# Attention and feed-forward on one core: the last 13 keys of each head as tiles of 32 rows, value products in four banks

## The reference

```python
def block(x, ctx):                                  # per batch
    xn = layernorm(layernorm(x)) * gamma + beta
    q, (k, v) = xn @ w_q, split(ctx @ w_kv)
    p = softmax(q_h @ k_h.T * 64 ** -0.5)           # per head h: 256 x 77
    x = x + (concat(p @ v_h) @ w_out + b_out) * tanh(gate)
    y = layernorm(x)
    h = silu(y @ (w_gate / 127).T) * (y @ (w_up / 127).T)   # 768 hidden
    return x + h @ (w_down / 127).T
```

## Time and profile before

| | us |
|---|---|
| median of 3 runs | 296.05 (295.01 to 296.74) |
| the profiled execution | 297.51 |
| its span | 295.7 |
| PE busy | 285.9 (97%) |
| DVE busy | 231.1 (78%) |
| ACT busy | 158.8 (54%) |
| POOL busy | 172.1 (58%) |
| PE, records of L849 (value products) in the chain that ended last | 10% |

### The profile page before, as it was taken

The page is one execution under the profiler, slowest core; times in us unless marked ns, Lnnn a source line. Parts: engine busy times, 40 slices in busy tenths (PEclk is TensorE's granted clock), DMA queues, the critical chain, the costliest instruction groups (busy, mean ns, idle before and its releaser), DMA issues.

```text
span 295.7 us, 6752 instructions
## 1 busy us (share of the span) xinstructions
PE 285.9 (97%) x2509; PEld 262.9 (89%) x2509; DVE 231.1 (78%) x609; ACT 158.8 (54%) x312; POOL 172.1 (58%) x198
## 2 busy tenths in 40 slices
PE   8999999979999999999999999999999999999895
PEld 7998978868988898989898989898999889988794
DVE  1598887777898789878987897788878878886853
ACT  4646875548268633853484358326842773354142
POOL 2653864358959681966396549635872778145033
PEclk9999999999999999999999999999999999999979
DMA  6995147332432113011201120112012101110001
GB/s 198 384 368 153 34 115 243 147 97 109 145 107 80 24 32 97 0 40 43 73 0 40 42 73 2 39 53 59 3 41 76 35 3 42 41 34 2 0 26 51
DMA packets 26668, 23.32 MB, mean 79 GB/s; under 512 B 12602, under 2 KB 24866, under 8 KB 26634
## 3 DMA queue, kind: packets, MB, share of 16 engines
q1 hardware_dynamic: 26634, 22.86, 24.9%
HBM read 15.87 MB, written 4.62 MB: 69 GB/s over the span
## 4 chain that ended last, share of the span: by engine, by line
PE 86%; DVE 6%; ACT 2%; issue 2%; SPq 1%; DMA 1%; POOL 1%; DVEq 0%
PE ps L904 13%; PE ps L849 10%; PE ps L808 6%; PE ps L816 5%; PE ps L812 5%; PE ps L973 5%; PE ps L977 5%; PE ps L974 5%; PE ps L738 5%; PE ps L831 4%; PE ps L957 3%; PE ps L960 3%; PE ps L925 2%; PE ps L771 1%; PE ps L746 1%
## 5 line engine op out<-in xcount | busy, mean ns | idle before, releaser
L1224 POOL TENSOR_TENSOR probs<-probs,total 128x512 f32<-128x512 f32 x32 | 33.6, 1049 | 59.6 <-DVE total L1363 59.5
L1250 POOL TENSOR_TENSOR h_lo<-hid,h_hi 128x256 fp32r<-128x256 f32 x42 | 30.9, 737 | 29.9 <-ACT h_hi L1137 29.5
L1239 POOL TENSOR_TENSOR t_lo<-t_all,t_hi 128x1232 fp32r<-128x1232 f32 x16 | 45.6, 2852 | 3.8 <-ACT t_hi L1095 3.8
L1067 ACT COPY pt<-ps 128x512 f32<-128x512 f32 x32 | 18.9, 591 | 40.8 <-PE ps L831 40.8
L973 PE MATMUL ps<-wo_hi,o_hi 128*128 128x256 f32 x128 | 36.3, 283 | 0.0
L974 PE MATMUL ps<-wo_lo,o_hi 128*128 128x256 f32 x128 | 36.1, 282 | 0.0
L977 PE MATMUL ps<-wo_hi,o_lo 128*128 128x256 f32 x128 | 36.0, 281 | 0.0
L1083 ACT CAST o_hi<-ps 128x512 fp32r<-128x512 f32 x32 | 17.2, 591 | 27.0 <-PE ps L849 27.0
L1346 DVE TENSOR_REDUCE top<-ps 128x4 f32<-128x308 f32 x64 | 28.7, 473 | 3.4 <-PE ps L816 3.1
L808 PE MATMUL ps<-t_hi,xn_hi 128*128 128x308 f32 x128 | 30.7, 321 | 0.0
L1371 DVE TENSOR_TENSOR o_lo<-ps,o_hi 128x512 fp32r<-128x512 f32 x32 | 20.6, 686 | 12.5 <-ACT o_hi L1083 12.2
(11 more groups left out here) (168 smaller groups left out, 838.2 us busy)
## 6 DMA issues: line engine op xcount, KB each, us to landing
x_ln<-in_x SPq DMA_DIRECT2D x8, 256.0 KB, 2.9
v_scratch<-v_out SPq DMA_DIRECT2D x4, 512.0 KB, 3.3
v_whole<-v_scratch SPq DMA_DIRECT2D x16, 128.0 KB
stream<-in_x SPq DMA_DIRECT2D x8, 256.0 KB, 2.9
x_rooms<-in_x SPq DMA_DIRECT2D x7, 256.0 KB, 7.7
out<-stream SPq DMA_DIRECT2D x7, 256.0 KB, 2.2
wk_raw<-in_L_xattn_w_kv SPq DMA_DIRECT2D x4, 256.0 KB, 5.2
wq_raw<-in_L_xattn_w_q SPq DMA_DIRECT2D x1, 1024.0 KB, 7.9
```

What stands on the lines that cost most here:

```text
L1224: nc.gpsimd.tensor_tensor(whole, whole, scale.to_broadcast([P, HR, HALVES, KEYS_WHOLE]), ALU.mult).then_inc(probs_done, 1)
L1239: nc.gpsimd.tensor_tensor(t_lo[:, :, cols], t_all[:, :, n, cols], t_hi[:, :, cols].bitcast(F32), ALU.subtract).then_inc(tlo_done, 1)
L1250: nc.gpsimd.tensor_tensor(h_lo[:, f, :], hid_of(b, f), h_hi[:, f, :].bitcast(F32), ALU.subtract).then_inc(hlo_done, 1)
```

## The change

The 13 remaining keys of heads 2j and 2j+1 of a group (halves r = 0 and 1) now stand together in 26 of the 32 rows from 32 j on, for j = 0 to 3. Head r's values are in the columns of half e = (r + j) % 2 and zeros in the other half. So a group's 8 rest products use 32 rows and 64 columns each, at eight places of the array. Pair j of a group has a bank of its own: j = 0 takes a bank of the shared ring (V0 and V1 become users of it), j = 1 to 3 take banks 3, 4 and 5. All 8 whole products come first, four and four, then the 8 rest products. The scores have two banks instead of three. o_hi and o_lo are read as 256 and 768 elements per partition instead of 512 twice, and the projection's waits follow. w_out is loaded by four DMAs instead of eight, with its rows in the new order. On DVE, Z2 stands ahead of LN. In the ring, banks are now X1T 6, V0 7, XT 2, G0 6, G1 7, G2 2, G3 6, G4 7, G5 2, V1 6, O0 7, O1 2, D0 6, D1 7; the last rounds have other banks in places.

```diff
-MISC_BANKS = (6, 7, 3)
-SCORE_BANKS = (0, 1, 2)
-LAST_BANKS = (4, 5, 7, 6, 0, 1)
-LAST_X1T_BANKS = (0, 2)
-LAST_DOWN_BANKS = (2, 3)
+MISC_BANKS = (6, 7, 2)
+SCORE_BANKS = (0, 1)
+VALUE_BANKS = (3, 4, 5)
+LAST_BANKS = (4, 5, 2, 6, 0, 1)
+LAST_X1T_BANKS = (0, 3)
+LAST_DOWN_BANKS = (3, 7)
+FORMER_GATE_BANK = 6
...
-DVE_ORDER = "LN1 M2 LN Z2 X1 M3 O0 H0 Z3 H1 H2 M0 H3 H4 O1 Z0 H5 M1 R0 Z1 R1 AG Y0 Y1".split()
+DVE_ORDER = "LN1 M2 Z2 LN X1 M3 O0 H0 Z3 H1 H2 M0 H3 H4 O1 Z0 H5 M1 R0 Z1 R1 AG Y0 Y1".split()
...
-V_BANKS = (4, 5, None, 2, 3, 4, 5, 4, 3, None)
+V_BANKS = (4, 5, None, 3, 7, 4, 5, 4, 3, None)
...
+    REST = P // HR
...
-        shared = [n for n in PE_ORDER if n in ("X1T", "XT", "G0", "G1", "G2", "G3", "G4", "G5", "D0", "D1", "O0", "O1")]
+        shared = [n for n in PE_ORDER if n in ("X1T", "XT", "V0", "V1", "G0", "G1", "G2", "G3", "G4", "G5", "D0", "D1", "O0", "O1")]
...
+                if n[0] == "V":
+                    return olo_done, NU * b + 2 * k + 1
...
+        def value_bank(g, j):
+            return bank[f"V{g}"] if j == 0 else VALUE_BANKS[j - 1]
...
+        def value_psum(g, i):
+            at = bank[f"V{g}"] if i == 0 else VALUE_BANKS[0]
+            return ps[:, at:at + (1 if i == 0 else HR - 1), 0:Q]
...
-                    first = r * KEYS_WHOLE + j * NEW
-                    sp.dma_start(v_rest[first:first + NEW, :, j * DH:(j + 1) * DH], by_head[rest_keys[r], r, j]).then_inc(v_in, 16)
+                    first, e = j * REST + r * NEW, (r + j) % 2
+                    sp.dma_start(v_rest[first:first + NEW, :, e * DH:(e + 1) * DH], by_head[rest_keys[r], r, j]).then_inc(v_in, 16)
...
-                if isinstance(b, int) and b == 0 and u == 1:
-                    evacuated(pe, first_v + V_BANKS.index(SCORE_BANKS[2]))
...
-                for pair in range(2):
-                    for keys in (v_whole, v_rest):
-                        for e in range(2):
-                            j = 2 * pair + e
-                            at = j if keys is v_whole else HR
-                            for r in range(HALVES):
-                                half = slice(r * KEYS_WHOLE, r * KEYS_WHOLE + (KEYS_WHOLE if keys is v_whole else HR * NEW))
-                                ins = mm(ps_p[e * DH:(e + 1) * DH, r, pair * Q:(pair + 1) * Q],
-                                         keys[half, g, j * DH:(j + 1) * DH], pt[half, at, :],
-                                         start=keys is v_whole, stop=keys is v_rest)
+                if isinstance(b, int) and b == 0 and g == 0:
+                    evacuated(pe, last_v)
+                claim(b, f"V{g}")
+                for turn in range(2):
+                    for r in range(HALVES):
+                        for j in range(HR):
+                            if (j // 2 + j + r) % 2 == turn:
+                                e = (r + j) % 2
+                                half = slice(r * KEYS_WHOLE, (r + 1) * KEYS_WHOLE)
+                                mm(ps[e * DH:(e + 1) * DH, value_bank(g, j), 0:Q],
+                                   v_whole[half, g, j * DH:(j + 1) * DH], pt[half, j, :], start=True, stop=False)
+                for e in range(2):
+                    for j in range(HR):
+                        part = slice(j * REST, j * REST + HALVES * NEW)
+                        ins = mm(ps[e * DH:(e + 1) * DH, value_bank(g, j), 0:Q],
+                                 v_rest[part, g, e * DH:(e + 1) * DH], pt[part, HR, :], start=False, stop=True)
                 ins.then_inc(pv_done, 1)
...
-                    if t == 0 and i % 2 == 0:
-                        pe.wait_ge(ohi_done, NU * b + i // 2 + 1)
+                    if t == 0 and i % HR < 2:
+                        pe.wait_ge(ohi_done, NU * b + 2 * (i // HR) + i % HR + 1)
...
-                    nc.scalar.copy(o_hi[:, 2 * n:2 * n + 2, :],
-                                   ps_p[:, i, :].rearrange("p (i q) -> p i q", i=2)).then_inc(ohi_done, 1)
+                    nc.scalar.copy(o_hi[:, value_chunks(g, i), :], value_psum(g, i)).then_inc(ohi_done, 1)
```

More of the change, by code:

```diff
@@ L120, in xattn_ffn_kernel @@
     V_LOADS = HALVES + HG
-    assert HALVES * KEYS_WHOLE == P and 0 < HR * NEW <= KEYS_WHOLE
+    REST = P // HR
+    assert HALVES * KEYS_WHOLE == P and 0 < HALVES * NEW <= REST and 1 + len(VALUE_BANKS) == HR
     assert HB * K <= BANK and DC == 2 and NT == 2 and 2 * DH == P and RC == VS + 1 and K <= P
@@ L298, in last_user @@
                 n, k = shared[at], int(shared[at][1]) if shared[at][1].isdigit() else 0
+                if n == "G5" and isinstance(b, int) and b == B - 1:
+                    at -= len(MISC_BANKS)
+                    continue
                 if n == "XT" and not (isinstance(b, int) and b >= B - 1):
                     return xn_done, DC * (b + 2)
+                if n[0] == "V":
+                    return olo_done, NU * b + 2 * k + 1
                 if n[0] == "O" and not (isinstance(b, int) and b == B):
@@ L406, in gate_up_psum, with value_chunks @@
         def gate_up_psum(b, f):
-            return ps[:, LAST_BANKS[f], :] if last(b) else ps[:, bank[f"G{f}"], :]
+            if last(b):
+                return ps[:, LAST_BANKS[f], :]
+            return ps[:, FORMER_GATE_BANK if b == B - 1 and f == FC - 1 else bank[f"G{f}"], :]
+        def value_bank(g, j):
[3 more added lines that the diff above has]
+            return ps[:, at:at + (1 if i == 0 else HR - 1), 0:Q]
+        def value_chunks(g, i):
+            return slice(HR * g, HR * g + 1) if i == 0 else slice(HR * g + 1, HR * (g + 1))
         def tile(t):
@@ L628, in _ @@
             sp.wait_ge(s_job, last_t + 1)
-            out_rows = w_out.rearrange("(g n e r d) m -> e g r d n m", g=2, e=2, r=HALVES, d=DH)
+            out_rows = w_out.rearrange("(i j r d) m -> j r d i m", j=2, r=HALVES, d=DH)
+            wo_pairs = wo_raw.rearrange("p (i j) m -> p j i m", j=2)
             def load_wo(*which):
-                for i in which:
+                for j in which:
                     for e in range(2):
-                        sp.dma_start(wo_raw[e * DH:(e + 1) * DH, 2 * i:2 * i + 2, :],
-                                     out_rows[e, i // HALVES, i % HALVES]).then_inc(s_in["wo"], 16)
+                        sp.dma_start(wo_pairs[e * DH:(e + 1) * DH, j], out_rows[j, (e + j) % 2]).then_inc(s_in["wo"], 16)
             load_ln(1)
-            load_wo(0, 1, 2)
+            load_wo(0)
             for r in range(RC):
@@ L644, in _ @@
                 if r == 0:
-                    load_wo(3)
+                    load_wo(1)
                 if r == 1:
@@ L911, in gate_up_last @@
                     pe.wait_ge(x2hi_done, B + 1)
-                if LAST_BANKS[f] == bank["G5"]:
+                if LAST_BANKS[f] == FORMER_GATE_BANK:
                     pe.wait_ge(hid_done, FC * (B - 1))
@@ L970, in project @@
                 for i in range(IC):
-                    if t == 0 and i % 2 == 0:
-                        pe.wait_ge(ohi_done, NU * b + i // 2 + 1)
+                    if t == 0 and i % HR < 2:
+                        pe.wait_ge(ohi_done, NU * b + 2 * (i // HR) + i % HR + 1)
                     mm(o, o_hi[:, i, ts], wo_hi[:, i, :], start=i == 0, stop=False)
                     mm(o, o_hi[:, i, ts], wo_lo[:, i, :], start=False, stop=False)
-                    if t == 0 and i % 2 == 0:
-                        pe.wait_ge(olo_done, NU * b + i // 2 + 1)
+                    if t == 0 and i % HR < 2:
+                        pe.wait_ge(olo_done, NU * b + 2 * (i // HR) + i % HR + 1)
                     ins = mm(o, o_lo[:, i, ts], wo_hi[:, i, :], start=False, stop=i == IC - 1)
@@ L1034, in wout_hi @@
             def wout_hi():
-                act.wait_ge(s_in["wo"], 16 * 4 * HALVES)
+                act.wait_ge(s_in["wo"], 16 * 4)
                 act.wait_ge(s_job, last_v + 1)
@@ L1230, in normalise @@
                 ends = bass.AP(at.tensor, at.offset, [at.ap[0], [NEXT, HR], [NEXT - NEW, HALVES], [1, NEW]])
-                to = rest[:, n % ROOMS, :].rearrange("p (r k) -> p r k", r=HALVES)[:, :, 0:HR * NEW]
-                nc.gpsimd.tensor_tensor(to.rearrange("p r (j k) -> p j r k", k=NEW), ends,
+                to = rest[:, n % ROOMS, :].rearrange("p (j k) -> p j k", j=HR)[:, :, 0:HALVES * NEW]
+                nc.gpsimd.tensor_tensor(to.rearrange("p j (r k) -> p j r k", r=HALVES), ends,
                                         scale.to_broadcast([P, HR, HALVES, NEW]), ALU.mult).then_inc(rest_done, 1)
@@ L1370, in split_o @@
                         wait(dve, proj_done, NT * b)
-                    nc.vector.tensor_tensor(o_lo[:, 2 * n:2 * n + 2, :],
-                                            ps_p[:, i, :].rearrange("p (i q) -> p i q", i=2),
-                                            o_hi[:, 2 * n:2 * n + 2, :].bitcast(F32), ALU.subtract).then_inc(olo_done, 1)
+                    nc.vector.tensor_tensor(o_lo[:, value_chunks(g, i), :], value_psum(g, i),
```

(1 more changed line is left out.)

## The result

The changed kernel takes **303.96 us** (median of 4 runs, 303.38 to 305.12) against 295.94 (295.01 to 296.74) for the kernel before in the same session: ratio 1.026, 95% interval 1.023 to 1.030. I had said 297.1, at most 300.0. The profiled execution took 303.38 us, its span is 301.6 and TensorE's granted clock 1.00 throughout.

The account below looks back on a forecast made before the run. TensorE, busy in all 28.53 us of a middle round, was taken as the bound. Round 0 -0.15, round 1 +0.50, middle rounds 0.0 and round 7 +0.73 gave +1.1 on 296.05, so 297.1 us, range 293.5 to 300.0.

Parts of the forecast that it names:

- The values stage: TensorE's value products: three steps instead of four, 0.43 less 0.15 for an added tile-shape change, saving 0.28 us, 16 times.
- rival D: Values stage: the eight tiles run in two steps, each stage 0.15 longer; +5.4 us, 301.4; chance 12%.
- over 0.6: Sign for the rest step of a values stage: the forecast is wrong if it takes over 0.6 us.
- rival B: Values stage: the added change of tile shape is free, 0.43 saved a stage; -0.1 us, 296.0; chance 13%.
- Wait 1: S3 on two score banks waits for DVE's subtraction of S2's first half: 0.20 us late each round, 0.73 in round 1.
- Wait 2: G1 on V0's bank waits for group 0's first o_lo on DVE: G1 +0.25 us, so V0's saving is gone.
- before 119.6: Sign in the middle round: the forecast is wrong if DVE's o_lo comes before 119.6 on the scale of before.
- Wait 3: V1 on G3's bank waits for H3's product, allowed at 127.92 where TensorE arrives at 127.88; it eats V1's saving.
- The closed sum of a middle round: V1 16.08 us after S2, then 12.46 to the next S2: period 28.54 against 28.53, five rounds 0.0.
- The ends: Rounds outside the middle five: round 0 -0.15 us, round 1 +0.50, round 7 +0.73.
- The sum: Whole kernel: -0.15 + 0.50 + 0.0 + 0.73 = +1.1 us, so 297.1 us.
- Rival C: G1's and V1's new waits cost nothing because H3 comes earlier; -2.6 us, 293.5; chance 15%.

Follow-up runs that it names:

- experiment 6: Kernel of 5 with DVE's M2 as maximum 0, subtraction 0, maximum 1, subtraction 1, instead of both maxima first: 296.48 us, 1.0007 of before.
- 10: Kernel of 9 with o_lo of the last round's second group ahead of H4 on DVE: 294.46 us, 0.9941 of before.
- experiment 4: The kernel before with two score banks instead of three, nothing else: 297.76 us, 1.008 of before.
- Experiment 3: The changed kernel, with P2 on POOL held back until LN's two instructions on DVE are done (rounds 0 to 6): 301.12 us, 1.0175 of before.
- experiment 1: The changed kernel with LN ahead of Z2 on DVE again, nothing else: 298.88 us, 1.012 of before.
- experiment 8: The changed kernel with DVE's new order kept and only POOL's bias moved behind h1: 302.44 us, 1.023 of before.
- 9: Kernel of experiment 7 with O0 of the last round in bank 1, the other score bank: 294.77 us, 0.9957 of before.
- experiment 7: Kernel of experiment 6 with round 7's V1 putting its first pair into score bank 0, waiting for S3's subtraction: 295.53 us, 0.9985 of before.
- 5: Kernel of experiment 1 with POOL's bias moved behind h1 in rounds 1 to 6: 296.35 us, 1.0008 of before.

## Why the prediction was wrong

**The values stage, right.** The eight tiles of 32 rows run together (rival D is out): the 16 records of L877 span 0.69, with 0.63 to the next stage, and the whole takes 1.65 where I had 1.90 - 0.28 = 1.62. My sign "over 0.6" for the rest step was set too tight, since this 0.63 holds the way out too (0.55 in the kernel before). So about 0.25 is saved; in the kernel without waits (experiments 6 to 10) two stages save 28.53 - 28.06 = 0.47, 0.235 each. What is missing to 0.43 is 0.18, against my 0.15 (rival B, a free change, is out). The traces do not tell a change of tile shape that costs 0.18 from a rest step that is itself longer.

**Wait 1, right.** S3 is 0.22 late (predicted 0.20), and experiment 4 shows it alone: 28.75 - 28.53. In round 1 I had 0.73: from V1 of round 0 to V0 of round 1 experiment 4 takes 16.95 us (70.67 to 87.62) where the kernel before takes 16.21 (71.66 to 87.87), +0.74.

**Wait 2, the step that failed:** "Now DVE idles there and LN's 0.64 comes after the reciprocal." I took LN's duration from where it had stood, where POOL did nothing. The reciprocal, which I named myself, releases P2 as well. Each of POOL's products reads two SBUF tensors, and x_hat goes from SBUF to SBUF. Beside P2 LN delays X1 by 119.19 - 117.84 = 1.35, not 0.64. From there the delay can be followed: o_lo at S2 + 8.46 instead of 7.70 (120.30 on the scale of before; my sign "before 119.6" stood above my own 119.54), G1 at S2 + 8.92 instead of 8.16. That is +0.76 for G1, of which 0.73 is the second x_hat (1.14 - 0.41); 0.28 of G0's waiting for X1 lies inside G1's wait. Experiment 3 gives LN 0.70 back by moving POOL only, and 0.70 of the round with it. The Trainium skill, "SBUF — State Buffer", section "SBUF: two separate sides", says that some DVE instructions and GpSimd share a pair of ports as an exclusive lock, held for the whole instruction. By that rule the second x_hat waits for P2's end, 119.12, and then takes its 0.41. The trace agrees in part: x_hat was held up, but ended at 119.27, 0.26 sooner than that; and P2, which started while the first x_hat ran, was 0.07 longer, not held until its end. Experiment 3 shows that P2 is the cause; that a lock on ports is the mechanism is not shown.

**Wait 3, right in place, wrong in size.** I held that H3 hangs on S2 alone and comes at S2 + 16.04. It hangs on o_lo too: M3 late makes G1 late, then t1 and the exponential of unit 3 on ACT, h0 on ACT and POOL (idle 1.22 for h_hi where it had been 0.44), then P3, the bias and h1. H3's product ends at 129.76, S2 + 16.89. Even without that delay, in experiment 1, V1 waits 0.34, since S3's 0.2 shifts this chain as well; and V1 starts 0.15 after the product ended, where I had 0.04. The closed sum of a middle round is V1 at S2 + 17.04 instead of 16.08, and from V1 to the next S2 12.52 instead of 12.46: 29.56 against 28.54. The 1.02 between them, six times, is nearly the whole miss. Which part is LN's is shown by experiment 1 (0.85 a round), and which is the bias's by experiment 8 (0.39); together they are more than 1.02 because with both gone the saving of the values stages comes out too.

**The ends.** Round 0 is a second miss, of 0.74 counted from V0: V0 to V1 grew from 9.25 us (62.41 to 71.66) to 10.12 (61.27 to 71.39), +0.87 where I had +0.13. V1 waits 0.6 there for DVE's copy into wu_t. I had moved that copy 0.28 earlier with V0's saving; counted from V0 it came 0.33 later (70.57 - 61.27 against 71.38 - 62.41). Part of this is no loss: V0 itself came 1.14 earlier, as it didn't wait for its DMA (0.88 in the kernel before). In experiments 6, 9 and 10, whose V0 waited for the DMA again, V0 to V1 is 9.58 or 9.59, +0.33. What holds the copy I did not test. Round 7 is nearly right: V1 starts 14.31 after S2 instead of 13.07, +1.24 where I had 1.01; the difference is the size of S3's 0.22, which my sum had not passed on to H3. From V0 to V1 it grew by 1.00 (8.50 to 9.50), and V1 waits 1.16 for H3. That O0 would wait for H4 as soon as this wait went, I did not see; experiment 7 paid 1.20 for it.

**The sum.** From V0 of round 0: 1.34 to V0 of round 1 (26.80 against 25.46), 6.1 for six rounds, 1.00 - 0.25 for round 7: 8.2 by the traces, 8.0 by the medians. Mine was 1.1. The miss of about 7 is 6.1 in the six rounds (in my sum they came to nearly nothing, counted from V0 to V0), 0.75 in round 0 and 0.2 in round 7.

**Rival C**, in which waits 2 and 3 cost nothing, is 293.5. It needed other orders: with LN back, the bias moved, M2 split and two banks of round 7 changed, the kernel is at 294.46, 294.37 at the full clock.

The steps with their medians and rounds:

| kernel | median us | median of the runs with a mean granted clock of 0.997 or more | round us |
|---|---|---|---|
| before | 295.94 | 295.57 to 295.98, three sessions | 28.53 |
| after | 303.96 | 303.84 (3 of 4) | 29.56 |
| 1: LN ahead of Z2 | 298.88 | 298.88 (4 of 4) | 28.71 |
| 5: and bias behind h1 | 296.35 | 296.34 (9 of 10) | 28.30 |
| 6: and M2 in turn | 296.48 | 295.17 (5 of 10) | 28.07 |
| 7: and V1 of round 7 in bank 0 | 295.53 | 295.39 (7 of 10) | 28.07 |
| 9: and O0 of round 7 in bank 1 | 294.77 | 294.31 (7 of 12) | 28.08 |
| 10: and o_lo ahead of H4 | 294.46 | 294.37 (8 of 12) | 28.06 |

Rows of different sessions differ by up to 0.4 us for that alone (the kernel before). What stays open is why the clock falls in 280 to 284 in some executions and not in others, of the same kernel too.

## What to carry to other kernels

An instruction that is moved keeps its duration only if its new neighbours on the other engines are like the old ones: before pricing it from its old row, look at what the same event releases elsewhere. When a resource gets more users in a ring, write down for each new wait the whole chain of its releaser; the moved LN cost 0.06 us a round with the old banks and 0.85 with the new ones (29.56 - 28.71). And a saving on the engine that bounds the kernel is worth its size only once every wait behind it has been moved: here 0.47 us a round came out only after three more edits of the order (experiments 1, 5 and 6), and the step from round 0 to round 1 still loses 1.0 us. Before a gain or loss of 1 us is put down to an edit, compare runs with the same granted clock: the edit of experiment 6 gained 1.2 us and its median showed nothing, that of experiment 7 gained nothing and its median fell by 0.95.

## What the runs showed of the hardware

- A DVE instruction from SBUF to SBUF (x_hat, 128x256, 0.41 us) took 1.14 us beside a POOL product of 128x512 (1.05 us alone, 1.12 beside it), and 0.38 when it started just ahead of that product.
- Eight fp32 matmuls on tiles of 32 rows by 64 columns, in four banks, run together: 0.69 us from the first start to the last end, and 0.63 to the next stage. A stage of three steps with them takes 1.65 us, one of four steps on 64 rows 1.90, which leaves 0.18 for the change from 64 to 32 rows or for a longer step.
- TensorE's clock was at the lower level for most of 4 us behind a stretch in which the engine had idled for 1.3 of 4 us (0.64 in 280 to 284 in experiment 6), and this cost 1.4 us. The same idling did not always bring it: experiment 1 idled 1.31 of 4 us in 280 to 284 and kept 1.00 behind it. Runs of one kernel with a mean clock of 0.993 or 0.994 took 1.4 us more than those at 0.998 or more in the kernel before (297.31 against 295.88), and 2.2 in experiment 6 (297.41 against 295.17).
